# Two dense attentions on one Trainium2 core: f32 row maxima turned as four strips between the next step's two maxima, and sums turned and divided once per unit

## The chip, the core and the metric

The kernel runs on one core of one Trainium2 chip. The metric is device time in microseconds of one whole execution; the three runs of the kernel before are compared by their median. The profile is one further execution of the same program, and all times inside the kernel come from it. TensorE is called PE in the rows (PEld is its weight load), VectorE DVE, ScalarE ACT, GpSimd POOL, and SyncE, which here only issues transfers, SP.

## The reference, cut to what matters

Two adaptive-layer-norm blocks follow each other; each has a dense attention with 16 heads of 8 channels over 2 x 1024 tokens, and another layer behind it. The first dense attention is plain, the second multiplies its probabilities by an upper triangle after the softmax:

```python
qk = jnp.einsum('bhqd,bhkd->bhqk', q, k)
qk = qk / jnp.float32(np.sqrt(s))
p = jax.nn.softmax(qk, axis=-1)
...
mask = jnp.triu(jnp.ones((s, s), dtype=p.dtype), k=0)
p = p * mask
z = jnp.einsum('bhqk,bhkd->bhqd', p, v)
```

Between the two attentions lie two windowed layers, and behind the second a four-round mixture of experts. None of these is touched by the change.

## The kernel before

Everything here is in `attention`, which is built twice (`att0` plain, the second one causal). A **unit** is four heads of one batch, 8 units in each attention; its queries are handled in two **halves** of 512. A **step** g is one tile of 128 keys against one half of the queries, for the four heads; so a half is 8 steps, a unit 16, an attention 128 steps.

In a step PE computes four score tiles (L806, keys on partitions, one bank each of three), ACT takes the exponential of each (L878), and one step later PE multiplies the probabilities with the values of the four heads, in four column strips of 32 (L824; in the causal attention also L827 for tiles that need only the sum, and L833 for the diagonal tile, after POOL has masked it). The softmax needs the row maximum of every query beforehand. For that PE computes the scores a second time with queries on partitions (L777, two matmuls of 512 columns for one **maximum**), into one of two 1024-wide buffers, the **ring**, and DVE reduces the buffer to one negated maximum per query (L889). Two maxima belong to each step; they run LEAD = 11 steps (22 maxima) ahead of the scores that use them. In a step the PE program alternates: score 0, first half of the even maximum, score 1, its second half, score 2, first half of the odd maximum, score 3, its second half, then the values of the step before. A score uses 50 rows of the array in one half, the maximum next to it 48 rows in the other, and the two are issued at nearly the same time.

When the 16 maxima of a half are complete, DVE splits them into two bf16 parts (L894, L896), PE turns them into rows by four matmuls with the identity (`rows`, L788) into a ring buffer, DVE copies the rows out (L904), and SP puts them with two transfers (L729) as extra rows of the query operand, so that the scores come out with the maximum subtracted. When the values of a half are complete, ACT copies the sums out of PSUM (`take_sums`, L870), PE transposes them in four 128x128 blocks into a ring buffer (`turn`, L797), and DVE takes the reciprocal of the denominators and multiplies (L913, L918).

The ring is one sequence for all three kinds (`order`, numbered by `number`): entry n lies in buffer n mod 2, and DVE drains the entries strictly in this order. PE waits at an entry's first matmul:

```python
if number[e] >= 2:
    pe.wait_ge(ring_free, number[e] - 1)
return ring[number[e] % 2]
```

so entry n may be written when entry n-2 has been drained. PE executes its program in the order written. `first` is the part before step 0: 22 maxima and the first `rows`.

Of the kernel before, what the change touches and what calls it, by code (L numbers as in the profile page):

```python
# [24 lines left out]
P = 128  # L25
# [613 lines left out]
def attention(nc, k, tag, scale, causal, operands, pool_aside=None):  # L639
# [8 lines left out]
    (hm_ready, ring_ready, ring_free, st_ready, exp_done, pv_done,  # L648
     v_staged, v_ready0, masked, evacuated, hi_done, rec_done, tri_loaded) = sems(
        nc, *(f"{tag}_{n}" for n in (  # L650
            "max_parts_ready", "ring_filled",
# [11 lines left out]
    with ctx:  # L663
# [10 lines left out]
        rec = sb("rec", [P, 4, GROUP])  # L674
# [23 lines left out]
        first = []  # L698
        for pair in range(LEAD):
            first += [("max", 2 * pair), ("max", 2 * pair + 1)]  # L700
            if pair == SEQ_TILES:
                first.append(("rows", 0))
        order = first + [e for g in range(LAST) for e in entries(g)] + [("turn", HALVES - 1)]
# [17 lines left out]
        @block.sync  # L721
        def _(sp):
            def rows(n):

                it, half = n // 2, n % 2
                sp.wait_ge(ring_free, number["rows", n] + 1)
                for p in range(2):
                    at = TILE_ROWS * p + MAX_ROW
                    sp.dma_start(q_op[it % RING][at:at + 2, :, half * CHUNK:(half + 1) * CHUNK],  # L729
                                 neg_rows[GROUP * p:GROUP * (p + 1), half * CHUNK:(half + 1) * CHUNK])\  # L730
                      .then_inc(m_rows[half], 16)

            def store_z(it):
                b, g = it // GROUPS, it % GROUPS

                sp.wait_ge(ring_free, number["turn", 2 * it + 1] + 1)
# [12 lines left out]
            sp.wait_ge(operands.stored[2], 16 * 2 * TERMS)  # L749
            for it in range(UNITS):  # L750
                rows(2 * it + 1)
                if it + 1 < UNITS:
                    rows(2 * it + 2)
                if it + RING < UNITS:
                    sp.wait_ge(exp_done, GROUP * STEPS * (it + 1))
                    operands.load(sp, it + RING)
                if causal and it:
                    store_z(it - 1)
            if causal:
                store_z(UNITS - 1)  # L760
                sp.wait_ge(z_stored, 16 * GROUP * UNITS)

        @block.tensor
        def _(pe):
# [19 lines left out]
            def rows(n):  # L784
                buf = claim(("rows", n))
                pe.wait_ge(hm_ready, n + 1)
                for t in range(4):
                    last = pe.matmul(buf[0:2 * GROUP, t * P:(t + 1) * P],  # L788
                                     neg_parts[:, n % 2 * 4 + t, :, :, :].rearrange("p a c j -> p (a c j)"),
                                     k.ident_bf[:, :], start=True, stop=True)  # L790
                last.then_inc(ring_ready, 1)

            def turn(n):
                buf = claim(("turn", n))
                pe.wait_ge(evacuated, n + 1)
                for t in range(4):
                    last = pe.transpose(buf[:, t * P:(t + 1) * P], sums[:, n % 2, t * P:(t + 1) * P], k.ident[:, :])  # L797
                last.then_inc(ring_ready, 1)
# [38 lines left out]
            def extras(found):  # L837
                for kind, arg in found:
                    if kind == "rows":
                        rows(arg)  # L840
                    if kind == "turn":
                        turn(arg)
# [8 lines left out]
            for g in range(LAST):  # L851
                it, half = g // STEPS, g // SEQ_TILES % 2
                if g % SEQ_TILES == 0:
                    pe.wait_ge(m_rows[half], 32 * (it + 1))
# [9 lines left out]
            turn(HALVES - 1)  # L864

        @block.scalar
        def _(act):
            def take_sums(n):
                act.wait_ge(pv_done, (n + 1) * SEQ_TILES)
                act.activation(sums[:, n % 2, :], out_bank, ACT.Copy).then_inc(evacuated, 1)  # L870
# [13 lines left out]
        def _(dve):  # L884
            def maximum(m):
# [3 lines left out]
                dve.tensor_reduce(neg[:, t, p, j:j + 1], ring[e % 2], AX.X, ALU.max, negate=True).then_inc(ring_free, 1)  # L889
                if (m + 1) % (2 * SEQ_TILES) == 0:  # L890
                    n = m // (2 * SEQ_TILES)
                    at = slice(n % 2 * 4, n % 2 * 4 + 4)
                    dve.wait_ge(ring_free, e + 1)
                    dve.tensor_copy(neg_parts[:, at, :, 0, :], neg[:, at, :, :]).then_inc(hi_done, 1)  # L894
                    dve.wait_ge(hi_done, n + 1)
                    dve.tensor_tensor(neg_parts[:, at, :, 1, :], neg[:, at, :, :], neg_parts[:, at, :, 0, :], ALU.subtract)\  # L896
                       .then_inc(hm_ready, 1)

            def rows(n):
                e, it, half = number["rows", n], n // 2, n % 2  # L900
                dve.wait_ge(ring_ready, e + 1)
                if it:
                    dve.wait_ge(m_rows[half], 32 * it)
                dve.tensor_copy(neg_rows[:, half * CHUNK:(half + 1) * CHUNK], ring[e % 2][0:2 * GROUP, 0:CHUNK])\  # L904
                   .then_inc(ring_free, 1)

            def turn(n):
                e, it, half = number["turn", n], n // 2, n % 2
                dve.wait_ge(ring_ready, e + 1)
                if n + 1 == HALVES:  # L910
                    dve.wait_ge(ring_free, e)
                tile = ring[e % 2][:, 0:CHUNK].rearrange("p (t h c) -> p t h c", t=4, c=32)
                dve.reciprocal(rec[:, :, :], tile[:, :, :, HEAD_DIM]).then_inc(rec_done, 1)  # L913
                dve.wait_ge(rec_done, n + 1)
                out = k.att[:, 4 * half:4 * half + 4, it, :].rearrange("p t (h c) -> p t h c", c=HEAD_DIM)
                num = tile[:, :, :, 0:HEAD_DIM]
                by = rec[:, :, :].unsqueeze(3).broadcast_to([P, 4, GROUP, HEAD_DIM])
                dve.tensor_tensor(out, num, by, ALU.mult).then_inc(ring_free, 1)  # L918

            for kind, arg in order:  # L920
# [8 lines left out]
        def _(pool):  # L929
            if causal:  # L930
# [1405 lines left out]
```

## Time and profile before

| | us |
|---|---|
| median of 3 runs | 1818.78 (1818.23 to 1824.21) |
| profiled execution, its own time | 1818.17 |
| profiled execution, span | 1816.0 |
| PE busy | 1563.5 (86%) |
| DVE busy | 1385.3 (76%) |
| ACT busy | 1193.3 (66%) |
| POOL busy | 637.7 (35%) |
| exponentials (L878), 1024 | 535.2 |
| reductions to maxima (L889), 512 | 600.9 |

The span is the time from the first to the last instruction; the profiled execution's own time is 2.2 us longer. The first attention's maxima begin at 83.7 us, its last division is at about 440 us; the second attention's lie at 987 and 1364 us. The granted PE clock is 1.00 of full speed in the bodies of both, and 0.50 where each begins. A busy share names no limit by itself: in both attentions PE, DVE and ACT are all busy for most of the time, and what sets the pace has to be read from the order and the waits.

### The profile page before, as it was taken

Reading aid. Unit: us, or ns where it says so; the run is one execution under the profiler, and the core shown is the slowest. Engines: PE = TensorE matmul, PEld = TensorE weight load, DVE = VectorE, ACT = ScalarE, POOL = GpSimd, SP = SyncE. Lnnn points to the kernel's source line nnn. Section 1 sums busy time; section 2 is a strip of 40 time slices with the busy share of each in tenths; the row PEclk is TensorE's granted clock in tenths of the full one; section 3 lists DMA queues with packets and bytes.
Section 4 is the critical chain, followed back from the end, with each engine's and each line's share of the span. In section 5 each row is a group of like instructions: output and inputs, shape, how many; then the busy total and the mean of one; then the engine's idle time right before and its main releaser. Section 6 shows DMA issues by size and latency. Waiting matters only on the chain. (4 is left out here: it accounts for less than half of the span.)

```text
span 1816.0 us, 29185 instructions
## 1 busy us (share of the span) xinstructions
PE 1563.5 (86%) x11008; PEld 854.3 (47%) x11008; DVE 1385.3 (76%) x1948; ACT 1193.3 (66%) x2306; POOL 637.7 (35%) x516
## 2 busy tenths in 40 slices
PE   6489999998579987799984999999985799999998
PEld 4112222222356664566741233333334577888886
DVE  3799999993577546875445999999935399999996
ACT  2338888887367743677533577777772578777776
POOL 1840000000377551776304122222222255555555
PEclk9669999999789987899986799999996899999999
DMA  2230000000111100111002301111002011111111
GB/s 74 64 128 19 19 19 19 19 2 1 68 30 31 31 24 18 27 33 32 5 6 83 111 19 22 22 22 22 5 7 73 21 56 42 47 47 43 46 47 53
DMA packets 66619, 66.03 MB, mean 36 GB/s; under 512 B 38920, under 2 KB 42632, under 8 KB 65968
## 3 DMA queue, kind: packets, MB, share of 16 engines
q1 hardware_dynamic: 65840, 61.94, 12.6%
q10 hardware_dynamic: 576, 2.16, 0.3%
q8 instruction: 88, 1.44, 0.3%
q14 instruction: 51, 0.42, 0.1%
q0 software_dynamic: 64, 0.07, 0.0%
HBM read 40.85 MB, written 14.81 MB: 31 GB/s over the span
## 5 line engine op out<-in xcount | busy, mean ns | idle before, releaser
L878 ACT ACTIVATE att_probs<-psum 128x512 f32<-128x512 f32 x1024 | 535.2, 602 | 201.4 <-PE psum L806 200.7
L889 DVE TENSOR_REDUCE att_neg_max<-psum 128x1 f32<-128x1024 f32 x512 | 600.9, 1219 | 44.4 <-PE psum L777 38.6
L777 PE MATMUL psum<-att_k_op,att_q_op 48*128 48x512 bf16 x1024 | 350.2, 408 | 56.5 <-DMA att_k_op<-qk_parts 34.8
L806 PE MATMUL psum<-att_q_op,att_k_op 50*128 50x512 bf16 x1024 | 313.5, 387 | 19.7 <-ACT att_probs L878 19.7
L1973 ACT ACTIVATE moe_hidden<-psum,moe_b 128x512 f32<-128x512 f32 x256 | 167.4, 690 | 83.2 <-PE psum L76 81.4
L69 DVE TENSOR_TENSOR moe_hidden_low<-moe_hidden,moe_hidden_high 128x512 fp32r<-128x512 f32 x192 | 202.5, 1103 | 5.4 <-ACT moe_hidden_high L1979 5.3
L824 PE MATMUL psum<-att_probs,att_v 128*32 128x512 f32 (+2 forms) x1664 | 203.2, 558 | 2.9 <-ACT att_sums L870 2.8
L806 PEld LDWEIGHTS psum<-att_q_op,att_k_op 50*128 50x128 bf16 x1024 | 78.1, 94 | 251.0 <-ACT att_probs L878 187.9
L965 POOL TENSOR_TENSOR att_diag<-att_probs,att_triangle 128x512 f32<-128x512 f32 x64 | 81.3, 1270 | 272.2 <-PE psum L827 176.7
L777 PEld LDWEIGHTS psum<-att_k_op,att_q_op 48*128 48x128 bf16 x1024 | 72.4, 95 | 180.6 <-DVE att_neg_max L889 120.4
L2034 POOL TENSOR_TENSOR moe_hidden_low<-moe_hidden,moe_hidden_high 128x512 fp32r<-128x512 f32 x64 | 94.5, 1477 | 168.2 <-ACT moe_hidden_high L1979 168.0
L1624 POOL TENSOR_TENSOR wl_qk<-wl_qk,wl_part 128x512 f32<-128x512 f32 x64 | 81.6, 1277 | 102.4 <-DVE wl_part L1503 102.4
L2029 POOL TENSOR_TENSOR moe_cur<-moe_cur,moe_term 128x512 f32<-128x512 f32 x64 | 105.4, 1647 | 13.4 <-DVE moe_term L2109 13.1
L74 PE MATMUL psum<-moe_hidden_high,moe_w_high 128*128 128x512 f32 x256 | 103.1, 403 | 6.5 <-DVE moe_hidden_low L69 6.5
L1979 ACT ACTIVATE moe_hidden_high<-moe_hidden 128x512 fp32r<-128x512 f32 x192 | 106.7, 625 | 0.0
L1520 DVE TENSOR_REDUCE wl_mx<-psum 128x4 f32<-128x512 f32 x64 | 44.1, 689 | 77.6 <-PE psum L1236 77.6
L74 PE MATMUL psum<-moe_cur_high,moe_w_high 128*128 128x512 f32 x256 | 101.0, 395 | 0.0
L75 PE MATMUL psum<-moe_hidden_low,moe_w_high 128*128 128x512 f32 x256 | 100.5, 392 | 0.0
L76 PE MATMUL psum<-moe_hidden_high,moe_w_low 128*128 128x512 f32 x256 | 100.3, 392 | 0.0
L76 PE MATMUL psum<-moe_cur_high,moe_w_low 128*128 128x512 f32 x256 | 99.8, 390 | 0.0
L75 PE MATMUL psum<-moe_cur_low,moe_w_high 128*128 128x512 f32 x256 | 99.6, 389 | 0.0
L954 POOL COPY att_v<-v_tok 128x256 f32<-128x256 f32 x16 | 6.4, 401 | 253.5 <-PE psum L824 253.5
(246 smaller groups left out, 2898.3 us busy)
## 6 DMA issues: line engine op xcount, KB each, us to landing
moe_spread_weights<-gate_rows SPq DMA_DIRECT2D x64, 256.0 KB, 3.2
wl_v_shift<-wl_v SPq DMA_DIRECT2D x62, 128.0 KB, 2.2
att_q_op<-qk_parts SPq DMA_DIRECT2D x32, 192.0 KB, 3.3
att_k_op<-qk_parts SPq DMA_DIRECT2D x32, 192.0 KB, 4.3
qk_parts<-att_hi SPq DMA_DIRECT2D x12, 256.0 KB
qk_parts<-att_hi SPq DMA_DIRECT2D x12, 192.0 KB
qk_parts<-att_mid SPq DMA_DIRECT2D x8, 256.0 KB
moe_w<-in_moe_w SPq DMA_DIRECT2D x2, 1024.0 KB, 8.5
```

Source lines behind the costliest of these rows:

```text
L69: return dve.tensor_tensor(dst, src, high.bitcast(F32), ALU.subtract)
L74: pe.matmul(out, w_high, x_high, start=start, stop=False)
L75: pe.matmul(out, w_high, x_low, start=False, stop=False)
L76: return pe.matmul(out, w_low, x_high, start=False, stop=stop)
L777: mm = pe.matmul(buf[:, half * CHUNK:(half + 1) * CHUNK], q_op[it % RING][at_rows(p, MAX_ROW), j, t * P:(t + 1) * P], k_op[it % RING][at_r ...
L806: pe.matmul(st_bank[e % 3], k_op[it % RING][at_rows(p, MAX_ROW + 2), j, t * P:(t + 1) * P], q_op[it % RING][at_rows(p, MAX_ROW + 2), j, ha ...
L824: last = pe.matmul(out[:, 0:full], stage_v[r][:, t, j, :], pr[:, 0:full], start=first_tile, stop=final and full == CHUNK, skip_group_check ...
L878: act.activation(probs[:, g % PB, h, :], st_bank[e % 3], ACT.Exp, scale=scale).then_inc(exp_done, 1)
L889: dve.tensor_reduce(neg[:, t, p, j:j + 1], ring[e % 2], AX.X, ALU.max, negate=True).then_inc(ring_free, 1)
L1973: act.activation(hidden[:, n % 2, f, :], k.psum[:, f, :], ACT.Gelu_apprx_tanh, bias=b1[:, e, f:f + 1]).then_inc(gelu_done, 1)
L1979: act.activation(hidden_high[:, n % 2, f, :], hidden[:, n % 2, f, :], ACT.Copy)\
L2029: pool.tensor_tensor(cur[:, at], cur[:, at], term[:, n % 2, :], ALU.add).then_inc(added, 1)
```

## The change

The maxima are kept as f32 in a tile of 16 columns for each of the 8 query tiles, of which 4 are used; POOL clears the tile once. `rows` turns them with four f32 matmuls against the f32 identity, each with 32 columns (two tiles of 16) as one column strip of 32; the strips 2 and 3 repeat the strips 0 and 1. The split into two bf16 parts is done when DVE takes the rows out of PSUM: one copy of 128x128, and one subtraction on the lower 64 partitions. The rows now lie as 128 columns on many partitions, so SP needs four transfers instead of two. The `rows` entry stands between the even and the odd maximum of its step, in `order` and in PE's program, where it was behind both. `turn` and the division are done once per unit, in the third step of the next unit, eight transposes and one 1024-wide ring buffer at a time, instead of once per half in the second step of the next half. The diff:

```diff
-        neg = sb("neg_max", [P, SEQ_TILES, 2, 2])
-        neg_parts = sb("neg_parts", [P, SEQ_TILES, 2, 2, 2], BF16)
-        neg_rows = sb("neg_rows", [2 * GROUP, SEQ], BF16)
+        neg = sb("neg_max", [P, SEQ_TILES, 16])
+        neg_rows = sb("neg_rows", [P, 2, P], BF16)
...
-                out += [("max", 2 * pair), ("max", 2 * pair + 1)]
+                out.append(("max", 2 * pair))
             if pair % SEQ_TILES == 0 and pair // SEQ_TILES - 1 < HALVES:
                 out.append(("rows", pair // SEQ_TILES - 1))
-            if g % SEQ_TILES == 1 and g > SEQ_TILES:
-                out.append(("turn", g // SEQ_TILES - 1))
+            if pair < LAST:
+                out.append(("max", 2 * pair + 1))
+            if g % STEPS == 2 and g > STEPS:
+                out.append(("turn", g // STEPS - 1))
...
                 for p in range(2):
-                    at = TILE_ROWS * p + MAX_ROW
-                    sp.dma_start(q_op[it % RING][at:at + 2, :, half * CHUNK:(half + 1) * CHUNK],
-                                 neg_rows[GROUP * p:GROUP * (p + 1), half * CHUNK:(half + 1) * CHUNK])\
-                      .then_inc(m_rows[half], 16)
+                    for j in range(2):
+                        at = TILE_ROWS * p + MAX_ROW
+                        sp.dma_start(q_op[it % RING][at:at + 2, j, half * CHUNK:(half + 1) * CHUNK],
+                                     neg_rows[2 * p + j::16, half, :])\
+                          .then_inc(m_rows[half], 16)
...
                 buf = claim(("rows", n))
-                pe.wait_ge(hm_ready, n + 1)
-                for t in range(4):
-                    last = pe.matmul(buf[0:2 * GROUP, t * P:(t + 1) * P],
-                                     neg_parts[:, n % 2 * 4 + t, :, :, :].rearrange("p a c j -> p (a c j)"),
-                                     k.ident_bf[:, :], start=True, stop=True)
+                pe.wait_ge(neg_cleared, 1)
+                pe.wait_ge(ring_free, number["max", 2 * SEQ_TILES * (n + 1) - 1] + 1)
+                for strip in range(4):
+                    t = n % 2 * 4 + strip % 2 * 2
+                    last = pe.matmul(buf[32 * strip:32 * strip + 32, 0:P],
+                                     neg[:, t:t + 2, :].rearrange("p t r -> p (t r)"), k.ident[:, :],
+                                     start=True, stop=True)
...
                 for i in range(GROUP):
                     score(g, i)
+                    if i == 2:
+                        for kind, n in entries(g):
+                            if kind == "rows":
+                                rows(n)
                     if pair < LAST:
                         maximum(2 * pair + i // 2, i % 2)
...
-                if (m + 1) % (2 * SEQ_TILES) == 0:
-                    n = m // (2 * SEQ_TILES)
-                    at = slice(n % 2 * 4, n % 2 * 4 + 4)
-                    dve.wait_ge(ring_free, e + 1)
-                    dve.tensor_copy(neg_parts[:, at, :, 0, :], neg[:, at, :, :]).then_inc(hi_done, 1)
-                    dve.wait_ge(hi_done, n + 1)
-                    dve.tensor_tensor(neg_parts[:, at, :, 1, :], neg[:, at, :, :], neg_parts[:, at, :, 0, :], ALU.subtract)\
-                       .then_inc(hm_ready, 1)
...
-                dve.tensor_copy(neg_rows[:, half * CHUNK:(half + 1) * CHUNK], ring[e % 2][0:2 * GROUP, 0:CHUNK])\
+                dve.tensor_copy(neg_rows[:, half, :], ring[e % 2][:, 0:P]).then_inc(hi_done, 1)
+                dve.wait_ge(hi_done, n + 1)
+                low = neg_rows[64:P, half, :]
+                dve.tensor_tensor(low, ring[e % 2][64:P, 0:P], low, ALU.subtract)\
                    .then_inc(ring_free, 1)
```

PE's program in the first attention, in the step in which the second `rows` falls (before: L806 score, L777 maximum, L824 values of four heads, L788 `rows`):

```order
L806 MATMUL psum<-att_q_op,att_k_op 128x512
L777 MATMUL psum<-att_k_op,att_q_op 128x512
L806 MATMUL psum<-att_q_op,att_k_op 128x512
L777 MATMUL psum<-att_k_op,att_q_op 128x512
L824 MATMUL psum<-att_probs,att_v_0 32x512 x4
L788 MATMUL psum<-ident_bf,att_neg_parts 8x128 x4
L806 MATMUL psum<-att_q_op,att_k_op 128x512
L777 MATMUL psum<-att_k_op,att_q_op 128x512
```

The same step in the changed kernel (L812 score, L780 maximum, L830 values, L793 `rows`):

```order
L812 MATMUL psum<-att_q_op,att_k_op 128x512
L780 MATMUL psum<-att_k_op,att_q_op 128x512
L812 MATMUL psum<-att_q_op,att_k_op 128x512
L780 MATMUL psum<-att_k_op,att_q_op 128x512
L812 MATMUL psum<-att_q_op,att_k_op 128x512
L793 MATMUL psum<-ident,att_neg_max 32x128 x4
L780 MATMUL psum<-att_k_op,att_q_op 128x512
L812 MATMUL psum<-att_q_op,att_k_op 128x512
L780 MATMUL psum<-att_k_op,att_q_op 128x512
L830 MATMUL psum<-att_probs,att_v_0 32x512 x4
```

`rows` has moved from behind the values to between score 2 and the odd maximum, with score 3 and the values behind it.

DVE's program of the first attention before, over one half and a little more:

```order
L904 CAST att_neg_rows<-psum 8x512
L889 TENSOR_REDUCE att_neg_max<-psum 128x1 x8
L913 RECIPROCAL att_rec<-psum 128x16
L918 TENSOR_TENSOR att<-psum,att_rec 128x4x32
L889 TENSOR_REDUCE att_neg_max<-psum 128x1 x6
L894 CAST att_neg_parts<-att_neg_max 128x8x2
L896 TENSOR_TENSOR att_neg_parts<-att_neg_max,att_neg_parts 128x8x2
L889 TENSOR_REDUCE att_neg_max<-psum 128x1 x2
```

And in the changed kernel, over one unit:

```order
L906 CAST att_neg_rows<-psum 128x128
L909 TENSOR_TENSOR att_neg_rows<-psum,att_neg_rows 64x128
L899 TENSOR_REDUCE att_neg_max<-psum 128x1 x11
L918 RECIPROCAL att_rec<-psum 128x32
L923 TENSOR_TENSOR att<-psum,att_rec 128x8x32
L899 TENSOR_REDUCE att_neg_max<-psum 128x1 x5
```

The two small split instructions are gone from between the maxima, the copy is wider in partitions and shorter in columns and has a subtraction behind it, and the division stands once in 32 maxima instead of twice.

## Rows read from the trace of the kernel before

**Rows 1.** The page, costliest groups: busy, mean ns, idle before.
```profile
L889 DVE TENSOR_REDUCE att_neg_max<-psum 128x1 f32<-128x1024 f32 x512 | 600.9, 1219 | 44.4 <-PE psum L777 38.6
```

**Rows 2.** Windows of one half each: length, busy PE, PEld, DVE, ACT, POOL, clock.
```profile
148.81:169.58 20.77, 20.07 (x137) 5.12 (x136) 20.13 (x21) 17.11 (x34) 0.40 (x1) 1.00 0.16 39
1117.75:1139.15 21.40, 20.48 (x144) 5.35 (x144) 20.76 (x22) 17.32 (x34) 2.53 (x2) 1.00 0.01 2
1139.15:1161.28 22.13, 20.59 (x240) 8.84 (x240) 20.22 (x22) 16.87 (x33) 8.34 (x8) 1.00 0.27 44
```

**Rows 3.** Timeline, an ordinary step of the first attention: start, length.
```profile
124.97 0.39 PE L806 MATMUL psum<-att_q_op,att_k_op 50*128 50x512 bf16 x1
125.39 2.06 ACT L878 ACTIVATE att_probs<-psum 128x512 f32<-128x512 f32 x4 [0.33 <-PE psum L806]
125.66 0.39 PE L777 MATMUL psum<-att_k_op,att_q_op 48*128 48x512 bf16 x1
126.05 0.39 PE L806 MATMUL psum<-att_q_op,att_k_op 50*128 50x512 bf16 x1
126.37 1.06 PE L824 MATMUL psum<-att_probs,att_v 128*32 128x512 f32 x8
127.36 0.39 PE L806 MATMUL psum<-att_q_op,att_k_op 50*128 50x512 bf16 x1
```

**Rows 4.** Timeline, behind rows, first attention.
```profile
129.96 0.39 PE L806 MATMUL psum<-att_q_op,att_k_op 50*128 50x512 bf16 x1
130.60 0.67 DVE L904 CAST att_neg_rows<-psum 8x512 bf16<-8x512 f32 x1
130.74 0.39 PE L777 MATMUL psum<-att_k_op,att_q_op 48*128 48x512 bf16 x1 [0.40 <-DVE att_neg_max L889]
131.33 0.39 PE L777 MATMUL psum<-att_k_op,att_q_op 48*128 48x512 bf16 x1
131.38 9.37 DVE L889 TENSOR_REDUCE att_neg_max<-psum 128x1 f32<-128x1024 f32 x8
131.86 1.06 PE L824 MATMUL psum<-att_probs,att_v 128*32 128x512 f32 x8
```

**Rows 5.** Timeline around a turn, and the group of another reciprocal.
```profile
137.72 0.39 PE L806 MATMUL psum<-att_q_op,att_k_op 50*128 50x512 bf16 x1
140.37 0.66 PE L797 MATMUL psum<-ident,att_sums 128*128 128x128 f32 x4
140.96 0.39 PE L806 MATMUL psum<-att_q_op,att_k_op 50*128 50x512 bf16 x1
141.06 0.26 DVE L913 RECIPROCAL att_rec<-psum 128x16 f32<-128x16 f32 x1 [0.31 <-PE psum L797]
141.35 0.29 DVE L918 TENSOR_TENSOR att<-psum,att_rec 128x128 f32<-128x128 f32 x1
...
L1516 DVE RECIPROCAL wl_stat<-wl_stat 128x64 f32<-128x64 f32 x8 | 4.4, 553 | 0.3
```

**Rows 6.** The start of the first attention: timeline, and one window.
```profile
100.52 5.45 POOL L1001 TENSOR_SCALAR lepe_term<-v_ch,lepe_taps 128x2046 f32<-128x2046 f32 x1
102.52 3.48 DVE L894 CAST att_neg_parts<-att_neg_max 128x16 bf16<-128x16 f32 x1
109.60 9.41 DVE L889 TENSOR_REDUCE att_neg_max<-psum 128x1 f32<-128x1024 f32 x8 [0.54 <-PE psum L777]
...
118.00:119.00 1.00, 1.00 (x8) 0.00 (x0) 1.00 (x1) 0.17 (x1) 0.00 (x0) 0.50 0.52 193
```

**Rows 7.** Timeline, causal attention: score 0 of three steps, each with a diagonal tile.
```profile
1135.29 0.39 PE L806 MATMUL psum<-att_q_op,att_k_op 50*128 50x512 bf16 x1
1141.65 0.39 PE L806 MATMUL psum<-att_q_op,att_k_op 50*128 50x512 bf16 x1
1144.29 0.39 PE L806 MATMUL psum<-att_q_op,att_k_op 50*128 50x512 bf16 x1
```

**Rows 8.** Line L729, the transfers of the maxima, both attentions: ns min/median/max.
```profile
L729 SPq DMA_DIRECT2D att_q_op<-att_neg_rows x64: 594/610/703, 109.1 to 1336.5; - x64
```

More of the change, by code:

```diff
@@ L699, in attention @@
         for pair in range(LEAD):
-            first += [("max", 2 * pair), ("max", 2 * pair + 1)]
+            first.append(("max", 2 * pair))
             if pair == SEQ_TILES:
                 first.append(("rows", 0))
-        order = first + [e for g in range(LAST) for e in entries(g)] + [("turn", HALVES - 1)]
+            first.append(("max", 2 * pair + 1))
+        order = first + [e for g in range(LAST) for e in entries(g)] + [("turn", UNITS - 1)]
         number = {e: n for n, e in enumerate(order)}
@@ L727, in rows @@
                 for p in range(2):
[L728 to L731 removed]
+                    for j in range(2):
[3 more added lines that the diff above has]
+                          .then_inc(m_rows[half], 16)
             def store_z(it):
                 b, g = it // GROUPS, it % GROUPS
[L736 removed]
+                sp.wait_ge(ring_free, number["turn", it] + 1)
                 for j in range(GROUP):
@@ L794, in turn @@
                 buf = claim(("turn", n))
-                pe.wait_ge(evacuated, n + 1)
-                for t in range(4):
-                    last = pe.transpose(buf[:, t * P:(t + 1) * P], sums[:, n % 2, t * P:(t + 1) * P], k.ident[:, :])
+                pe.wait_ge(evacuated, 2 * n + 2)
+                for t in range(SEQ_TILES):
+                    last = pe.transpose(buf[:, t * P:(t + 1) * P], sums[:, t // 4, t % 4 * P:(t % 4 + 1) * P],
+                                        k.ident[:, :])
                 last.then_inc(ring_ready, 1)
@@ L853, in _ @@
                 if g % SEQ_TILES == 0:
-                    pe.wait_ge(m_rows[half], 32 * (it + 1))
+                    pe.wait_ge(m_rows[half], 64 * (it + 1))
                 pair = g + LEAD
@@ L863, in _ @@
             values(LAST - 1)
-            turn(HALVES - 1)
+            turn(UNITS - 1)
         @block.scalar
@@ L869, in take_sums @@
                 act.wait_ge(pv_done, (n + 1) * SEQ_TILES)
+                if n >= 2:
+                    act.wait_ge(ring_ready, number["turn", n // 2 - 1] + 1)
                 act.activation(sums[:, n % 2, :], out_bank, ACT.Copy).then_inc(evacuated, 1)
@@ L888, in maximum @@
                 dve.wait_ge(ring_ready, e + 1)
[L889 to L897 removed]
+                dve.tensor_reduce(neg[:, t, 2 * p + j:2 * p + j + 1], ring[e % 2], AX.X, ALU.max, negate=True).then_inc(ring_free, 1)
             def rows(n):
@@ L902, in rows @@
                 if it:
-                    dve.wait_ge(m_rows[half], 32 * it)
-                dve.tensor_copy(neg_rows[:, half * CHUNK:(half + 1) * CHUNK], ring[e % 2][0:2 * GROUP, 0:CHUNK])\
+                    dve.wait_ge(m_rows[half], 64 * it)
+                dve.tensor_copy(neg_rows[:, half, :], ring[e % 2][:, 0:P]).then_inc(hi_done, 1)
+                dve.wait_ge(hi_done, n + 1)
+                low = neg_rows[64:P, half, :]
+                dve.tensor_tensor(low, ring[e % 2][64:P, 0:P], low, ALU.subtract)\
                    .then_inc(ring_free, 1)
             def turn(n):
-                e, it, half = number["turn", n], n // 2, n % 2
+                e = number["turn", n]
                 dve.wait_ge(ring_ready, e + 1)
-                if n + 1 == HALVES:
+                if n + 1 == UNITS:
                     dve.wait_ge(ring_free, e)
-                tile = ring[e % 2][:, 0:CHUNK].rearrange("p (t h c) -> p t h c", t=4, c=32)
+                tile = ring[e % 2].rearrange("p (t h c) -> p t h c", t=SEQ_TILES, c=32)
                 dve.reciprocal(rec[:, :, :], tile[:, :, :, HEAD_DIM]).then_inc(rec_done, 1)
                 dve.wait_ge(rec_done, n + 1)
-                out = k.att[:, 4 * half:4 * half + 4, it, :].rearrange("p t (h c) -> p t h c", c=HEAD_DIM)
+                out = k.att[:, :, n, :].rearrange("p t (h c) -> p t h c", c=HEAD_DIM)
                 num = tile[:, :, :, 0:HEAD_DIM]
-                by = rec[:, :, :].unsqueeze(3).broadcast_to([P, 4, GROUP, HEAD_DIM])
+                by = rec[:, :, :].unsqueeze(3).broadcast_to([P, SEQ_TILES, GROUP, HEAD_DIM])
                 dve.tensor_tensor(out, num, by, ALU.mult).then_inc(ring_free, 1)
+            dve.wait_ge(neg_cleared, 1)
             for kind, arg in order:
@@ L929, in _ @@
         def _(pool):
+            pool.memset(neg[:, :, :], 0.0).then_inc(neg_cleared, 1)
             if causal:
```

8 lines of the change are left out of this document (3 added, 5 removed).

## The prediction

> **What bounds the kernel now.** I read the page's groups first: 512 reductions of 1.22 us [rows 1] look like the limit of both attentions. The windows of one half each are next [rows 2]: in the first attention every half takes 20.77 us, with PE busy for 20.07, DVE for 20.13 and ACT for 17.11. So two engines are full, and only the timeline can tell which closes the loop.
>
> It shows a loop without DVE [rows 3]. Call the start of score 0 of a step S (124.97). Its exponential starts at S+0.42. Score 3 waits for that exponential's bank and goes at S+1.08. The values follow at S+1.40, and the next score 0 at S+2.39. A step thus cannot be shorter than 2.39 us, however fast DVE is. DVE needs 2 x 1.17 = 2.34 us for its two maxima (8 in 9.37 us, [rows 4]); it trails by a hair and fills its time, but does not set the step.
>
> The half then sums up on PE: 8 x 2.39 = 19.12; the step in which ACT also copies the sums is 0.26 longer (137.72 to 140.37 is 2.65, [rows 5]); the turn takes 0.59 (140.37 to 140.96); what is left of 20.77 is **0.80 for one `rows`**. I can place it: from 127.36 [rows 3] to 129.96 [rows 4] is 2.60, so 0.21 for the four small matmuls; then the first maximum of the next step waits for DVE until 130.74, 0.5 us late, with score 1 queued behind it; 0.08 is lost a step later. So DVE reaches into PE's chain only there.
>
> In the causal attention a step with a diagonal tile has a floor of 2.64 (1141.65 to 1144.29, [rows 7]). A unit is 21.40 + 22.13 = 43.53 [rows 2]; 8 x 2.39 + 8 x 2.64 + 2 x 0.26 + 2 x 0.59 = 41.94, so two `rows` cost 1.59 there. The one between 1135.29 and 1141.65 costs 6.36 - 2 x 2.64 = 1.08, the other 0.51.
>
> **The change, part by part.**
>
> *The place of `rows`.* Now it takes the ring entry between the even and the odd maximum of one step. The odd maximum may be written when the even one of the *same step* is drained, where in an ordinary step it needs only the odd one before. The even maximum's second half is issued at S+0.22 and takes 0.39, so DVE starts on it at about S+0.67 and releases it at S+0.67+1.22 = S+1.89; PE sees that at about S+1.94. Score 3, which was free at S+1.08, stands behind this wait in PE's program, and behind it are the rest of the odd maximum, the values, and the next step. Where a maximum and score 3 start late together, the values follow 0.53 after (131.33 to 131.86, [rows 4]) and the next step 0.99 after that: S+3.46. The step is 3.46-2.39 = **1.07 longer**, in both attentions, and nothing gives it back, since the steps after it are at PE and ACT's floor already. Against before that is +0.27 for each `rows` of the first attention, +0.56 and -0.01 for the two kinds of the second. `rows` 1 to 14 of each attention meet this (0 lies ahead of the steps, and for 15 there are no maxima left to block): 14 x 0.27 = **+3.8**, and 7 x 0.55 = **+3.9**.
>
> *The f32 matmuls of `rows`.* The trace has no four strips against the identity; the four transposes of 128x128 took 0.59 [rows 5], four bf16 ones 0.21. They run between S+0.7 and S+1.9, when PE waits anyway: nothing, at either price. Only above 1.15 us would they show.
>
> *The split on DVE.* It now follows the even maximum: a copy of 128x128 from PSUM and a subtraction on 64 partitions. Nearest is the 0.29 of the 128x128 multiply [rows 5]; the ends are that and twice the 0.67 of a 512-wide copy [rows 4]. I take 0.27+0.03+0.29 = 0.59: from S+1.84 to S+2.43, while the odd maximum is ready at about S+2.6. Hidden. At 1.35 it would delay the odd maximum and cost about 0.2 in the following step, 28 times: +5. What is removed from DVE, the two small split steps and the 0.67 copy, was worth time only by the 0.5 us wait that is already in the sum.
>
> *Turn and division.* PE issues eight transposes at once instead of twice four: 1.11 to 1.18 instead of 2 x 0.59. DVE's reciprocal over 32 columns lies between 0.26 (16) and 0.55 (64) [rows 5], I take 0.36, and 0.43 for the doubled multiply. The ring is free again 0.9 to 1.0 us into the next step instead of 0.7, which costs up to 0.1 there. Together 1.22 against 1.18: 14 x 0.04 = **+0.5**.
>
> *The start.* In the first attention the split before the first `rows` lasted 3.48 us instead of 0.17, and it ended just when POOL's 5.45 us instruction did (105.97, [rows 6]); DVE is the only limit there, since no scores run yet. The new order gives: last maximum of the half done at 102.49, next maximum to 103.7, split to 104.3, the odd maximum refilled (0.43 a matmul at the half clock, about 1.1 after its buffer is free) and reduced to 106.05. The next starts there instead of at 109.60: **-3.5**. The second attention has no such long split; the same sum gives **-0.2**.
>
> That copy reads PSUM now. By the Trainium skill, "VectorE: DVE Perf Modes", section "Why PSUM operands drop a tier", the fast two-port mode needs both SBUF read ports and a PSUM operand excludes it; "GPSIMD Engine Reference", section Specifications, names that mode as what contends with GpSimd. By this rule the stall cannot come back in the new copy, and the trace agrees as far as it goes, since the PSUM copy kept 0.67 us everywhere. Were it wrong, the 3.5 us would be lost again.
>
> *Ends and transfers.* In the last steps of each attention `rows` 15 saves 0.21 and one turn 0.59; the final turn and division are longer by about 0.5 and 0.2: zero. SP issues four transfers of 0.61 us [rows 8] instead of two. The split is done at S+2.43, the scores that need the rows start at S+3.46+2 x 2.39 = S+8.24; four issues take 2.4, which leaves 3.4 us for the last one to land. SP has nothing else to do then. Clearing the maxima's tile on POOL is over before the first matmul arrives.
>
> **Sum:** 3.8+3.9+0.5-3.5-0.2 = +4.5 us on the profiled execution's 1818.17, so 1822.7. The median of the runs is 0.6 above that execution; I forecast **1823.3**, +0.25%. A measurement of this kernel tells about 0.3%, 5.5 us, from no change.
>
> **The rivals.**
>
> *DVE sets the pace (faster).* If the loop of [rows 3] only looks closed and PE follows DVE, the time goes with DVE's work. Beyond 16 x 1.17 us a half has 2.0 us on DVE; afterwards 0.6 for the split and about 0.7 for half a turn with its wait. That saves 0.6 for each of 28 halves, 17, and 3.7 at the starts: 1798. For it: DVE's 20.13 of 20.77 [rows 2]. Against it: score 3's wait is for ACT, and PE's sum comes out to the hundredth. It wins only if the ring's wait can be passed by score 3. Chance 0.15.
>
> *The delay spreads (slower).* The blocked step starves DVE, and split and turn together run at their upper prices, so that the odd maximum or the one after the turn comes late: the point is a split above 0.9 us. Place: the step behind each `rows`. +0.2 x 28 on top of the sum: 1829. Chance 0.2.
>
> *The start gives more.* The clock is granted at 0.50 in the first scores [rows 6] and until 121; with PE no longer idle for 4 us before them it could rise earlier in its work. Two steps there took 7 instead of 4.8 us, so up to -2.5, which is 1821 down to 1818 with a cheaper turn. Chance 0.15.
>
> *The forecast itself:* 0.5, with its own range 1819 to 1828.
>
> **How the numbers follow.** The range 1811 to 1830 leaves out the first rival and a little above the second. Faster by over 0.3% (below 1813.3) is the first rival and a little: 0.16. Slower by over 0.3% (above 1824.2) is the second rival and some 0.2 of the forecast's 0.5: 0.39. The rest, 0.45, is within 0.3%.
>
> **What would show it.** In the changed kernel: steps with `rows` of about 3.46 us from score 0 to score 0 (3.7 with a diagonal tile), with PE idle for 0.8 us in front of the odd maximum, released by the even maximum's reduction; no wait of the first maximum of the next step; halves of 21.0 us on average in the first attention; DVE idle for 0.3 to 0.4 us after the odd maximum. The first reduction behind the first `rows` pair starts 3.5 us earlier. Wrong would be: steps below 2.35 us anywhere (then ACT and PE were not the floor), a split above 0.9 us, or a long copy beside POOL.

## The result, and the profile after

The changed kernel takes 1822.68 us in the median of 20 runs (1819.45 to 1827.07), the kernel before 1819.12 in 20 runs (1813.41 to 1824.42). The ratio is 1.002, with a 95% interval of 1.0011 to 1.0029: 3.6 us more. That is on the side that was forecast, and less than the 0.3% that the prediction took as the least difference to be told.

The profiled execution took 1827.07 us, its span is 1825.3. That is 9.3 longer than the span before, and 5.2 of it lie outside the two attentions, in stages that the change doesn't touch: they differ by some us from one execution to the next. So in what follows a kernel's **attention time** is read from its trace: from the start of the first reduction to a maximum to the end of the last division, for each attention, added up. For the changed kernel these are the starts of the first L899 and the ends of the last L923 in the timeline of DVE:

```profile
87.48 2.35 DVE L899 TENSOR_REDUCE att_neg_max<-psum 128x1 f32<-128x1024 f32 x2 [9.62 <-PE psum L780]
...
452.93 0.42 DVE L923 TENSOR_TENSOR att<-psum,att_rec 128x256 f32<-128x256 f32 x1
...
990.80 2.36 DVE L899 TENSOR_REDUCE att_neg_max<-psum 128x1 f32<-128x1024 f32 x2 [16.36 <-PE psum L780]
...
1370.97 0.42 DVE L923 TENSOR_TENSOR att<-psum,att_rec 128x256 f32<-128x256 f32 x1
```

That is 365.87 + 380.59 = 746.46 us, against 365.11 + 377.23 = 742.34 before: **+4.1**, where the forecast's sum was +4.5. (Before, the first attention's last division ends at 448.8 us, and not at about 440.)

The page's row of the reductions shows the new wait of DVE for maxima, 66.8 us where [rows 1] have 38.6:

```profile
L899 DVE TENSOR_REDUCE att_neg_max<-psum 128x1 f32<-128x1024 f32 x512 | 605.5, 1219 | 71.1 <-PE psum L780 66.8
```

The windows of one half each (columns as in [rows 2]) run from one copy of the rows to the next, two in the first attention and two in the causal one:

```profile
150.16:171.80 21.64, 20.04 (x144) 5.38 (x144) 20.11 (x22) 17.12 (x34) 0.40 (x1) 1.00 0.16 37
171.80:192.29 20.49, 19.05 (x136) 4.53 (x136) 19.42 (x19) 17.11 (x34) 0.00 (x0) 1.00 0.01 2
1053.80:1077.34 23.54, 20.99 (x256) 9.15 (x256) 20.12 (x22) 17.12 (x34) 9.56 (x9) 1.00 0.17 36
1077.34:1097.84 20.50, 19.06 (x136) 4.53 (x136) 19.43 (x20) 17.11 (x34) 1.27 (x1) 1.00 0.00 1
```

The first of each pair holds the turn of a unit, the second none; in the causal attention the first also holds all the diagonal tiles. A unit of the first attention is 42.13 us, 41.54 before; one of the second 44.04, 43.53 before. DVE no longer fills its time: 19.42 of 20.49 us in a half without the turn, where it was 20.13 of 20.77.

The timeline of the blocked step, which stands for [rows 4] now:

```profile
127.84 0.39 PE L812 MATMUL psum<-att_q_op,att_k_op 50*128 50x512 bf16 x1
128.63 0.43 PE L793 MATMUL psum<-ident,att_neg_max 128*32 128x128 f32 x8
129.66 0.28 DVE L906 CAST att_neg_rows<-psum 128x128 bf16<-128x128 f32 x1
129.80 0.39 PE L780 MATMUL psum<-att_k_op,att_q_op 48*128 48x512 bf16 x1 [0.75 <-DVE att_neg_max L899]
129.97 0.29 DVE L909 TENSOR_TENSOR att_neg_rows<-psum,att_neg_rows 64x128 bf16<-64x128 f32 x1
130.33 1.06 PE L830 MATMUL psum<-att_probs,att_v 128*32 128x512 f32 x8
130.44 1.22 DVE L899 TENSOR_REDUCE att_neg_max<-psum 128x1 f32<-128x1024 f32 x1 [0.17 <-PE psum L780]
131.33 0.39 PE L812 MATMUL psum<-att_q_op,att_k_op 50*128 50x512 bf16 x1
...
132.00 2.36 DVE L899 TENSOR_REDUCE att_neg_max<-psum 128x1 f32<-128x1024 f32 x2 [0.34 <-PE psum L780]
133.73 0.39 PE L812 MATMUL psum<-att_q_op,att_k_op 50*128 50x512 bf16 x1
```

Read it from S = 127.84. The four strips (eight matmuls in the trace) cost PE 0.43, in time in which it would wait anyway. The odd maximum is let in at S+1.96, released by the even maximum's reduction; the values follow at S+2.49, the next score 0 at S+3.49, and the step after that is back at 2.40. The split, 0.60 from 129.66 to 130.26, is over 0.17 before the odd maximum is there.

The turn, now eight transposes, holds PE for 1.02 (164.06 to 165.08), and the step after it is 2.51 instead of 2.39, its first maximum let in by the division:

```profile
164.06 1.09 PE L802 MATMUL psum<-ident,att_sums 128*128 128x128 f32 x8
165.08 0.39 PE L812 MATMUL psum<-att_q_op,att_k_op 50*128 50x512 bf16 x1
165.19 0.36 DVE L918 RECIPROCAL att_rec<-psum 128x32 f32<-128x32 f32 x1 [0.49 <-PE psum L802]
...
166.06 0.39 PE L780 MATMUL psum<-att_k_op,att_q_op 48*128 48x512 bf16 x1 [0.15 <-DVE att L923]
167.59 0.39 PE L812 MATMUL psum<-att_q_op,att_k_op 50*128 50x512 bf16 x1
```

And the start of the first attention, beside [rows 6]:

```profile
103.37 5.45 POOL L1008 TENSOR_SCALAR lepe_term<-v_ch,lepe_taps 128x2046 f32<-128x2046 f32 x1
107.43 0.28 DVE L906 CAST att_neg_rows<-psum 128x128 bf16<-128x128 f32 x1
...
108.64 3.58 DVE L899 TENSOR_REDUCE att_neg_max<-psum 128x1 f32<-128x1024 f32 x3 [0.60 <-PE psum L780]
```

The copy out of PSUM takes 0.28 in the middle of POOL's 5.45 us instruction, where the old SBUF copy took 3.48.

### The profile page after: what moved, and what is told of

It reads as the page before. It is cut to its first block and busy times, and to the rows that moved or that the text cites. A ratio compares the mean times of both kernels' runs of the same rounds, so it can differ in the third digit from the quotient of the medians.

```text
span 1825.3 us, 29457 instructions
## 1 busy us (share of the span) xinstructions
PE 1553.1 (85%) x11136; PEld 851.0 (47%) x11136; DVE 1366.9 (75%) x1884; ACT 1193.1 (65%) x2306; POOL 636.6 (35%) x518
## 5 line engine op out<-in xcount | busy, mean ns | idle before, releaser
L899 DVE TENSOR_REDUCE att_neg_max<-psum 128x1 f32<-128x1024 f32 x512 | 605.5, 1219 | 71.1 <-PE psum L780 66.8
L780 PE MATMUL psum<-att_k_op,att_q_op 48*128 48x512 bf16 x1024 | 345.6, 408 | 68.1 <-DMA att_k_op<-qk_parts 34.9
L812 PE MATMUL psum<-att_q_op,att_k_op 50*128 50x512 bf16 x1024 | 309.5, 387 | 30.8 <-ACT att_probs L888 30.7
L812 PEld LDWEIGHTS psum<-att_q_op,att_k_op 50*128 50x128 bf16 x1024 | 76.3, 94 | 298.8 <-ACT att_probs L888 245.4
L830 PE MATMUL psum<-att_probs,att_v 128*32 128x512 f32 (+2 forms) x1664 | 203.4, 558 | 2.9 <-ACT att_sums L880 2.8
L780 PEld LDWEIGHTS psum<-att_k_op,att_q_op 48*128 48x128 bf16 x1024 | 72.5, 95 | 165.9 <-DVE att_neg_max L899 114.2
```

Source lines behind the costliest of these rows:

```text
L780: mm = pe.matmul(buf[:, half * CHUNK:(half + 1) * CHUNK], q_op[it % RING][at_rows(p, MAX_ROW), j, t * P:(t + 1) * P], k_op[it % RING][at_r ...
L812: pe.matmul(st_bank[e % 3], k_op[it % RING][at_rows(p, MAX_ROW + 2), j, t * P:(t + 1) * P], q_op[it % RING][at_rows(p, MAX_ROW + 2), j, ha ...
L830: last = pe.matmul(out[:, 0:full], stage_v[r][:, t, j, :], pr[:, 0:full], start=first_tile, stop=final and full == CHUNK, skip_group_check ...
L899: dve.tensor_reduce(neg[:, t, 2 * p + j:2 * p + j + 1], ring[e % 2], AX.X, ALU.max, negate=True).then_inc(ring_free, 1)
```

## The experiments

The sum came out, but a sum of five terms can do that by luck, and one of them ("what is removed from DVE ... was worth time only by the 0.5 us wait") prices two edits as one. Seven kernels take them apart. Attention times, and the ratio of the medians to the kernel before, which was run again beside e1 to e4 (1818.78 us, 23 runs) and beside e5 to e7 (1819.81, 17 runs):

| kernel | first | causal | sum | ratio to before (95%) |
|---|---|---|---|---|
| before | 365.11 | 377.23 | 742.34 | |
| changed | 365.87 | 380.59 | 746.46 | 1.0011 to 1.0029 |
| e1, rows behind | 359.11 | 371.63 | 730.74 | 0.9918 to 0.9957 |
| e2, place alone | 374.51 | 392.41 | 766.92 | 1.0104 to 1.0142 |
| e3, turn per half | 365.39 | 380.64 | 746.03 | 1.0003 to 1.0028 |
| e4, longer split | 365.51 | 380.77 | 746.28 | 0.9992 to 1.0017 |
| e5, start apart | 367.15 | 377.18 | 744.33 | 1.0001 to 1.0025 |
| e6, values between | 379.73 | 382.08 | 761.81 | 1.0103 to 1.0138 |
| e7, split alone | 358.43 | 371.57 | 730.00 | 0.9908 to 0.9934 |

**e1: the changed kernel with `rows` back behind both maxima and the values.**

```diff
-                out.append(("max", 2 * pair))
+                out += [("max", 2 * pair), ("max", 2 * pair + 1)]
...
-            if pair < LAST:
-                out.append(("max", 2 * pair + 1))
...
                 for kind, arg in found:
+                    if kind == "rows":
+                        rows(arg)
...
-                    if i == 2:
-                        for kind, n in entries(g):
-                            if kind == "rows":
-                                rows(n)
```

> The changed kernel with one thing undone: the rows entry stands behind both maxima and behind the values again, in the ring's order and in PE's program; f32 strips, the split at the copy and the turn once per unit stay. Theory (the odd maximum's wait for the even one of its own step costs 1.07 to 1.10 us per rows, 28 times): rows then cost PE about 0.36 for the strips plus about 0.1 of waiting, 0.45 instead of 1.1, so 28 x 0.65 = 18 us less than the changed kernel: about 1804 to 1806, ratio to the kernel before 0.992. Rival (the place does not matter; the f32 strips, the wider split or the turn cost the 3.6 us): 1822, ratio 1.002.

Measured: 1808.61 us (6 runs; before 1818.78), ratio 0.9937, unit 40.92 in the first attention (21.03 + 19.89) and 42.55 in the causal one. The place of `rows` costs the changed kernel 15.7 us of attention time, 14 in the medians. The theory stands, 2 to 4 us short of its 18: `rows` cost 0.51 here and not 0.45, and one half early in each attention is 1.3 and 0.9 us longer than its like, by a wait that comes back in e7.

**e2: the kernel before with only the place changed.** Its diff is e1's the other way round, on the kernel before: bf16 parts, L904's copy and turn per half stay.

> The kernel before with the place alone changed: rows between the even and the odd maximum, with the bf16 parts, the 0.67 us copy, the 3.5 us stall at the start and the turn once per half as before. Theory: the same blocked step of 3.4 to 3.5 us, +0.27 and +0.55 us per rows, so +7.7 us and a little for the longer copy on DVE: 1826 to 1829, ratio 1.0042 to 1.0055. Rival (DVE's work sets the pace, which is unchanged): ratio 1.000.

Measured: 1843.79 us (4 runs), ratio 1.0123: 15 us above the expectation, a clear miss. DVE's timeline around one `rows`:

```profile
194.29 0.18 DVE L899 CAST att_neg_parts<-att_neg_max 128x16 bf16<-128x16 f32 x1
194.50 0.17 DVE L901 TENSOR_TENSOR att_neg_parts<-att_neg_max,att_neg_parts 128x16 bf16<-128x16 f32 x1
194.59 1.22 DVE L894 TENSOR_REDUCE att_neg_max<-psum 128x1 f32<-128x1024 f32 x1
195.72 0.67 DVE L909 CAST att_neg_rows<-psum 8x512 bf16<-8x512 f32 x1
196.50 1.23 DVE L894 TENSOR_REDUCE att_neg_max<-psum 128x1 f32<-128x1024 f32 x1
```

The split stands ahead of the even maximum whose end lets the odd one in. It delays this end by 0.33, and the blocked step by as much: 1.40 instead of 1.07. A half is then 19.12 + 0.26 + 0.59 + 1.40 = 21.37, and it measured 21.37. In the causal attention the two kinds differ: where the steps ahead are 2.64 long DVE has time for the split (it is idle for 0.28 in each), and the blocked step costs 1.14 (3.53 against 2.39); where POOL masks a diagonal tile at the same time the copy L899 takes 0.79, and it costs 1.97 (4.61 against 2.64). A unit is 45.02. That is 14 x 0.60 + 7 x 1.49 = 18.8 of the 24.6 us of attention time. Of the other 5.8, about 3.5 is a loss of clock (1.2 in each of three halves), below. What I had missed: moving the split out from between the maxima and moving `rows` in between them are bound to each other, and each alone has a price of its own.

**e3: the changed kernel with turn and division per half,** as before.

```diff
-            if g % STEPS == 2 and g > STEPS:
-                out.append(("turn", g // STEPS - 1))
+            if g % SEQ_TILES == 1 and g > SEQ_TILES:
+                out.append(("turn", g // SEQ_TILES - 1))
...
```

The rest of the edit gives `turn` its four transposes back and the division its four tiles.

> The changed kernel with the turn and the division once per half as before (four transposes, 0.26 + 0.29 us on DVE, in the second step of the next half). Theory: once per unit costs PE 1.03 + 0.12 = 1.15 us, twice per unit 2 x 0.59 = 1.18, so no difference: within 1.5 us of the changed kernel, ratio to before 1.0015 to 1.0028. Rival (division once per unit is a gain of its own, 0.3 us of DVE time and more per unit): 3 to 5 us slower than the changed kernel, ratio 1.004 to 1.005.

Measured: 1821.96 us (11 runs), every half of the first attention 21.09, against a mean of 21.07; a causal unit 44.07, against 44.04. Once per unit or per half is the same.

**e4: the changed kernel with one more subtraction in the split.**

```diff
                 low = neg_rows[64:P, half, :]
+                dve.tensor_tensor(spare[64:P, :], ring[e % 2][64:P, 0:P], low, ALU.subtract)
```

> The changed kernel with one more subtraction of 64x128 (0.29 us) on DVE in each of the 32 splits, its result unused. Theory (the split is hidden behind PE's refill of the odd maximum, 0.17 us of slack, and the next wait behind it has 0.3): at most 1 us more than the changed kernel. Rival (DVE sets the pace): 32 x 0.32 = 10 us more, ratio to before 1.007.

Measured: 1819.75 us (12 runs), attention time 0.2 less than without it. The median is 2.9 us below the changed kernel's; the attentions do not show that, so a difference of this size between two such medians is not read as an effect. DVE's timeline:

```profile
188.75 0.28 DVE L907 CAST att_neg_rows<-psum 128x128 bf16<-128x128 f32 x1
189.07 0.29 DVE L910 TENSOR_TENSOR att_spare<-psum,att_neg_rows 64x128 bf16<-64x128 f32 x1
189.28 0.29 DVE L911 TENSOR_TENSOR att_neg_rows<-psum,att_neg_rows 64x128 bf16<-64x128 f32 x1
189.60 1.23 DVE L900 TENSOR_REDUCE att_neg_max<-psum 128x1 f32<-128x1024 f32 x1
191.10 6.01 DVE L900 TENSOR_REDUCE att_neg_max<-psum 128x1 f32<-128x1024 f32 x5 [0.27 <-PE psum L781]
```

The odd reduction starts 0.85 behind the copy instead of 0.78; 0.07 of the 0.34 idle time behind it is used up, and nothing arrives later. So DVE's work at this place is not what the time goes with.

**e5: the kernel before, POOL's convolution held back until the first split is done.**

```diff
             if pool_aside is not None:
+                pool.wait_ge(hm_ready, 1)
                 pool_aside(pool)
```

> The kernel before, with one wait added: GpSimd's instruction of 5.45 us at the start of each attention begins only when the first split of the maxima is done. Theory (the 3.48 us of that 128x16 copy came from GpSimd's instruction beside it): the copy takes 0.17 to 0.18 us, the first attention's chain starts 3.3 us earlier (361.8 us from first reduction to last division, against 365.1), nothing else moves, since GpSimd's result is used far later: 1815.5 us, ratio 0.998. Rival 1 (the length is that of a first execution, not of a neighbour): the copy keeps about 3.4 us, ratio 1.000. Rival 2 (the neighbour moves onto something else): the copy is short, and another instruction of VectorE grows by about 3 us: ratio 1.000.

Measured: 1821.72 us (12 runs), ratio 1.0013, where 0.998 was expected: a miss. The first half of the theory holds, and the rival of a slow first execution falls: the first copy took 0.17 (at 104.11), and from the first reduction to the one behind the first `rows` it is 22.62 us instead of 25.92. But POOL's instructions now run until 130, into the second split. First DVE, then POOL, then PE:

```profile
126.62 3.35 DVE L894 CAST att_neg_parts<-att_neg_max 128x16 bf16<-128x16 f32 x1
...
125.42 4.53 POOL L1005 TENSOR_TENSOR lepe<-lepe,lepe_term 128x2046 f32<-128x2046 f32 x1
...
131.50 0.59 PE L788 MATMUL psum<-ident_bf,att_neg_parts 128*8 128x128 bf16 x4 [3.09 <-DVE att_neg_max L889]
```

and the windows, with PE's busy time first and the granted clock third from the end:

```profile
127.00:129.00 2.00, 1.42 (x11) 0.25 (x10) 2.00 (x1) 1.44 (x3) 2.00 (x1) 1.00 0.52 202
129.00:131.00 2.00, 0.00 (x0) 0.00 (x0) 1.97 (x3) 0.00 (x0) 1.28 (x2) 1.00 0.06 25
131.00:133.00 2.00, 1.49 (x7) 0.53 (x8) 2.00 (x3) 0.34 (x1) 0.00 (x0) 0.50 0.00 0
```

The copy ends with POOL's instruction once more (129.97 and 129.95; in [rows 6] both end at about 106). I had named the stall moving to another instruction of DVE as a rival; it moved to the same instruction's next turn. There it is dearer, since PE is at work: PE stands still for 3 us, the granted clock falls from 1.00 to 0.50, and the 3.3 won at the start are lost with 2 more.

**e6: e1 with the values of the step before between the even maximum and score 2,** in ordinary steps.

```diff
+                mid = g and g % SEQ_TILES != 1 and not (causal and 0 <= (g - 1) % SEQ_TILES - 4 * ((g - 1) // SEQ_TILES % 2) < 4)
                 for i in range(GROUP):
+                    if i == 2 and mid:
+                        values(g - 1)
...
-                if g:
+                if g and not mid:
```

> The changed kernel with the rows back behind both maxima (as in e1) and the values of the step before moved between the even maximum and score 2, in ordinary steps; left as they are in the first step of a half and after steps with a diagonal tile. Theory (a step of 2.39 is closed by PE and ACT: score, exponential, bank): ACT has its probabilities early enough, PE's work of a step is about 2.2 us, and the pace of these steps goes to VectorE's 2.35 for two maxima: up to 0.04 us for some 190 steps, minus 4 to 8 us against e1, so 1801 to 1805. Rival (the loop only turns round, since score 2 now stands behind the values and its exponential comes later): steps of 2.4 to 2.6, so 0 to +30 us against e1.

Measured: 1841.01 us (5 runs), ratio 1.0120, 31 us of attention time more than e1; the theory fell and the rival stands. The timeline of one turn of the loop (the L809 here are score 2 of a step and the next):

```profile
263.90 0.39 PE L809 MATMUL psum<-att_q_op,att_k_op 50*128 50x512 bf16 x1
264.32 2.07 ACT L886 ACTIVATE att_probs<-psum 128x512 f32<-128x512 f32 x4 [0.49 <-PE psum L809]
265.46 1.06 PE L827 MATMUL psum<-att_probs,att_v 128*32 128x512 f32 x8
266.46 0.39 PE L809 MATMUL psum<-att_q_op,att_k_op 50*128 50x512 bf16 x1
```

Score 2, 0.42 to its exponential, two exponentials (1.04), 0.10 to the values, 1.00 for these: 2.56. The values now wait for the probabilities of scores that were issued just ahead of them. DVE does exactly the work of e1, and the step is 0.17 longer: 21 us in the first attention. So the loop of PE and ACT sets the step, as the forecast said; but it was not open at the place where I cut it.

**e7: the kernel before with only the f32 strips and the split at their copy;** `rows` behind both maxima, turn per half.

```diff
-                if (m + 1) % (2 * SEQ_TILES) == 0:
...
-                    dve.tensor_copy(neg_parts[:, at, :, 0, :], neg[:, at, :, :]).then_inc(hi_done, 1)
-                    dve.wait_ge(hi_done, n + 1)
-                    dve.tensor_tensor(neg_parts[:, at, :, 1, :], neg[:, at, :, :], neg_parts[:, at, :, 0, :], ALU.subtract)\
...
-                dve.tensor_copy(neg_rows[:, half * CHUNK:(half + 1) * CHUNK], ring[e % 2][0:2 * GROUP, 0:CHUNK])\
+                dve.tensor_copy(neg_rows[:, half, :], ring[e % 2][:, 0:P]).then_inc(hi_done, 1)
+                dve.wait_ge(hi_done, n + 1)
+                low = neg_rows[64:P, half, :]
+                dve.tensor_tensor(low, ring[e % 2][64:P, 0:P], low, ALU.subtract)\
...
```

> The kernel before with only the f32 strips and the split at their copy; rows stand behind both maxima and the values, and turn and division are per half, both as before. Theory (what e1 gained was the removal of two small instructions and the shorter copy in front of the next even maximum, and the turn per unit is worth nothing): the same as e1, unit of 40.9 us in the first attention (41.5 before), ratio to the kernel before 0.993 to 0.995, 1807 to 1810. Rival (the turn once per unit made part of e1's gain, now that rows no longer fill the gap): 3 to 5 us more than e1, 1812.

Measured: 1806.27 us (5 runs), ratio 0.9921, a little below the 1807 to 1810 that were expected: faster than both kernels, and no slower than e1. The window of one half, and the timeline around one `rows`:

```profile
210.93:231.42 20.49, 20.04 (x141) 5.19 (x140) 19.77 (x22) 17.01 (x33) 0.00 (x0) 1.00 0.00 1
```
```profile
189.78 0.40 PE L790 MATMUL psum<-ident,att_neg_max 128*32 128x128 f32 x8
190.12 0.39 PE L808 MATMUL psum<-att_q_op,att_k_op 50*128 50x512 bf16 x1
190.45 0.28 DVE L898 CAST att_neg_rows<-psum 128x128 bf16<-128x128 f32 x1
190.59 0.39 PE L777 MATMUL psum<-att_k_op,att_q_op 48*128 48x512 bf16 x1
190.77 0.29 DVE L901 TENSOR_TENSOR att_neg_rows<-psum,att_neg_rows 64x128 bf16<-64x128 f32 x1
```

The first maximum behind `rows` goes 0.47 after score 0 (190.12 to 190.59), where it was 0.78 in [rows 4], and a half is 20.48 instead of 20.77: `rows` costs 20.48 - 19.12 - 0.26 - 0.59 = 0.51. What that maximum waits for is the reduction ahead of it, and that now starts without the two small instructions in front. Not all is won: early in the first attention scores wait once for the rows' transfers (1.34 us at 133.73), and in the causal one too (1.09 at 1032.36). SP issues them 2 us behind the split. Its waits from 117 to 135 us say why:

```profile
SPq L729 <- DMA qk_parts<-att_lo: 2.1, 1, 2.1
```

In SP's program these transfers stand behind a wait for the stores of the second batch's operands to land. The causal attention has the same wait of SP, 1.9 us. So another queue in program order holds back 1.1 to 1.4 us of the gain in each attention.

**Together.** With e7's split in place, putting `rows` between the two maxima costs 0.6 us a half (0.51 to 1.10) in the first attention and 16 us of attention time in all (e3 against e7, which differ in nothing else). The split alone is worth 12.3, of which about 4 come at the starts (22.28 us from the first reduction to the one behind the first `rows`, where it was 25.92, and 0.3 in the causal attention). The change is the sum of a loss and a gain of nearly the same size.

## Why the prediction was right

- **The loop of PE and ACT sets the step.** Supported from three sides: ordinary steps are still 2.39, although DVE is idle for 2.6 us of a unit in the first attention (42.13 - 20.11 - 19.42) instead of 1.3; e4 gives DVE more work for nothing; e6 changes only PE's order, and time follows.
- **The blocked step, S+3.46.** Measured S+3.49 (3.71 with a diagonal tile, 3.7 forecast), with PE idle 0.75 ahead of the odd maximum and no wait of the first maximum of the next step. Half without turn: 19.12 + 0.26 + 1.10 = 20.48, measured 20.49.
- **The strips and the split, hidden.** 0.43 and 0.60 (0.59 forecast), both covered. I had taken the odd maximum to be ready at about S+2.6; it was (130.44), so the cover was 0.17 and another 0.34 behind it.
- **The turn, 1.22 against 1.18.** Measured 21.64 - 20.49 = 1.15; e3 shows no difference. The term of +0.5 was too high: 14 x (1.15 - 1.18) is -0.4.
- **The start, -3.5 and -0.2.** From the first reduction to the first even one behind `rows` (108.64 and one reduction more, 109.82) it is 22.34 instead of 25.92: -3.6. Taking seven units at +0.59 and +0.51 from the attention times leaves -3.4 and -0.2.
- **Sum.** First attention +0.8 (forecast +0.55, with half of the turns), causal +3.4 (+3.95), together +4.1 (+4.5); in medians +3.6. Part of the closeness is luck. The turn's slip was made up by the place in the first attention (0.31 a `rows`, from 42.13 - 41.54 and the turn's -0.03, against 0.27). And the changed kernel, e3 and e4 have the same attention time to 0.5 us, yet their medians spread from 1819.75 to 1822.68: the attention times test the sum, the whole kernel's median does so only to some 3 us.

For the stall the prediction leant on the Trainium skill, "VectorE: DVE Perf Modes", section "Why PSUM operands drop a tier": a PSUM operand keeps an instruction out of the mode that needs both SBUF read ports. What hangs on that rule came out: here the PSUM copy kept 0.28 beside POOL's instruction, and in e5 the SBUF copy grew to 3.35 beside another one. The Trainium skill's "GPSIMD Engine Reference", section Specifications, which the prediction gives with that mode alone, also names VectorE instructions with two SBUF inputs. The new subtraction has one SBUF input and one from PSUM, and it kept 0.29 to 0.30 beside the same POOL instruction.

**What was incomplete** was the working of one term. "+0.27 for each `rows`" is right as a difference of the two programs, but it is no price of the place. By the runs it is +0.59 for the place and about -0.3 for taking two small instructions (0.33 with their gaps) out from between two maxima. The step "what is removed from DVE ... was worth time only by the 0.5 us wait that is already in the sum" joined the two: true for this sum, and wrong as soon as one is done without the other. It led straight to e2's expectation, which missed by 15 us, and it hid that the better half of the change could be had alone.

It also left a stall unseen. The prediction looked for long copies at the starts alone, and priced the causal attention's two `rows` at 1.08 and 0.51 without asking why. In the kernel before, ahead of each of the seven dear ones, the 128x16 copy runs beside POOL's masking of a diagonal tile:

```profile
1135.46 1.27 POOL L965 TENSOR_TENSOR att_diag<-att_probs,att_triangle 128x512 f32<-128x512 f32 x1 [22.13 <-PE psum L827]
...
1135.96 0.80 DVE L894 CAST att_neg_parts<-att_neg_max 128x16 bf16<-128x16 f32 x1
```

It takes 0.80 instead of 0.17 and ends 0.03 us behind that instruction (1136.76 and 1136.73). With the split out of PSUM (e7) the dear `rows` falls from 1.08 to 0.19 (a step of 2.83 against 2.64), the other one hardly, and a causal unit gains 0.94 where one of the first attention gains 0.57. No run takes this stall away by itself, so its share is read from the rows and not measured.

Of the rivals, DVE as the pace is refuted by e4 and e6. (Its 0.6 us a half should have been 0.7 by its own numbers, 2.0 less 0.6 and 0.7; that moves its 1798 by 3 us and no chance.) The spreading delay did not come: at 0.82 us (e4) the split was still free; its point of 0.9 was not tried. The start gave no more than its 3.6: the clock is granted in full from 123, 35 us behind the first reduction, and before from 122, 38 behind; so it came earlier only by as much as the work did. The two steps that were to gain took 7.6 us, and 7.4 before.

## What to carry to other kernels

A step that waits in an in-order queue costs what stands behind it in program order: follow the engine's program from the blocked entry to the next step, and the loss comes out to a few hundredths. When a change has one edit that removes work ahead of a wait and another that moves the wait, price each alone as well as both: a small instruction costs nothing on an engine with slack, and its full length when it stands ahead of the one reduction that another engine waits for. And moving a neighbour that slows an instruction helps only if its new place is looked at as well.

## What had not been expected of the hardware

- **A clock lost in a pause of about 1 us.** In e2's causal attention PE waits 0.99 and 0.66 us close together, in the seven halves in which the copy L899 takes 0.79. In three of these the granted clock fell (around 1063, 1200 and 1337); the first two then took 24.2 us where others take 23.0. Windows of e2:

```profile
1058.00:1060.00 2.00, 2.00 (x15) 0.39 (x15) 1.97 (x3) 1.67 (x4) 0.58 (x1) 1.00 0.03 8
1060.00:1062.00 2.00, 0.45 (x5) 0.23 (x4) 1.97 (x4) 1.25 (x3) 0.68 (x1) 1.00 0.00 0
1062.00:1064.00 2.00, 1.89 (x11) 0.48 (x15) 1.87 (x3) 0.60 (x1) 0.78 (x1) 0.74 0.01 2
1064.00:1066.00 2.00, 2.00 (x20) 0.52 (x12) 0.21 (x1) 0.67 (x2) 0.52 (x1) 0.50 0.01 3
```

  PE was busy for 0.45 of 2 us, and the level then went from 2.4 to 1.2 GHz for 3 to 4 us. The same pause in the other four halves left it at 1.00, and so did the single wait of 0.75 in the changed kernel. What decides between them stays open.
- **A copy of 128x16 that lasts as long as its neighbour.** SBUF to SBUF, f32 to bf16: 0.17 alone, 3.48 at the start of the kernel before and 0.80 in seven causal halves of it, 3.84 and 0.79 in the same places of e2, 3.35 in e5. Each time it ends within 0.04 us of POOL's instruction. The copy from PSUM of eight times the columns took 0.28 or 0.29 in all 32 places of the changed kernel.
